# Rows of a pass sent as soon as a buffer is free, the temperature as a factor of q's way out of its bank, and four last pieces split

## The reference, cut to what matters

```
x = norm(x + attention0(x))    # 16 heads of 8 channels, over all 1024 keys
x = norm(x + quantised_matmul(x))
x = norm(x + attention1(x))    # 16 heads of 8, layernorm of q and k, rope, causal
x = norm(x + ffn(x))           # silu(x Wg) * (x Wu), then Wd, hidden 384
```

```
q = l2norm(q) * scale;  k = l2norm(k) * scale
attn = softmax((q @ k.T) / temperature)
```

## Time and profile before

| | |
|---|---|
| time, median of 3 runs | 862.54 us (862.5 to 862.57) |
| profiled execution: its own time | 866.08 us |
| profiled execution: span from first to last instruction | 864.4 us |
| TensorE matmuls busy | 831.2 us, 96% |
| ScalarE busy | 771.8 us, 89% |
| VectorE busy | 550.9 us, 64% |
| GpSimd busy | 150.1 us, 17% |
| mean granted TensorE clock | 0.989 of full |

### The profile page before, as it was taken

One profiled execution on the slowest core, in us unless ns is written; L12 is line 12 of the kernel. 1 busy time (PEld: TensorE's weight loads), 2 busy tenths in 40 slices (PEclk: granted clock), 3 DMA queues, 4 the chain that ended last, 5 costly groups with the idle time before them and its releaser, 6 DMA issues.

```text
span 864.4 us, 16509 instructions
## 1 busy us (share of the span) xinstructions
PE 831.2 (96%) x6266; PEld 307.4 (36%) x6268; DVE 550.9 (64%) x1459; ACT 771.8 (89%) x864; POOL 150.1 (17%) x352
## 2 busy tenths in 40 slices
PE   8899999999999899999999999999999999989995
PEld 4232333333333333333333433343333443434444
DVE  6264666668758567787672576765563476765656
ACT  4899999999999799899899999999999998979851
POOL 3000000000001400034100410023200442352210
PEclk9999999999999899999999999999999999989998
DMA  5755513314432611352340321142140330062000
GB/s 152 246 160 184 171 38 115 105 37 158 161 122 76 218 38 61 111 184 74 134 160 25 111 98 38 61 160 74 38 159 25 98 112 25 26 221 85 1 13 27
DMA packets 48565, 88.60 MB, mean 103 GB/s; under 512 B 5088, under 2 KB 14432, under 8 KB 48480
## 3 DMA queue, kind: packets, MB, share of 16 engines
q1 hardware_dynamic: 48000, 87.00, 29.9%
q10 hardware_dynamic: 480, 0.48, 0.2%
HBM read 51.03 MB, written 35.65 MB: 100 GB/s over the span
## 4 chain that ended last, share of the span: by engine, by line
PE 80%; DVE 11%; DMA 3%; issue 3%; SPq 2%; ACT 1%; POOL 1%; DVEq 0%; ACTq 0%; POOLq 0%
PE ps L907 39%; PE ps L885 24%; PE ps L853 5%; PE ps L864 3%; PE ps L860 3%; PE ps L779 3%; DMA q_st<-parts_scratch 2%; PE ps L838 2%; ACT probs L757 1%; DVE th L1310 1%; DVE hT L1311 1%; SPq L540 1%; DVE sums_t L1151 1%; DVE mid_part L1300 1%; DVE mid_part L1301 1%
## 5 line engine op out<-in xcount | busy, mean ns | idle before, releaser
L757 ACT ACTIVATE probs<-ps 128x1024 f32<-128x1024 f32 x800 | 751.7, 1073 | 58.3 <-PE ps L885 55.6
L907 PE MATMUL ps<-probs,v_st 128*32 128x512 f32 (+3 forms) x3584 | 430.4, 562 | 3.4 <-issue 1.2
L885 PE MATMUL ps<-q_st,k_st 32*128 32x512 f32 (+3 forms) x1792 | 269.7, 462 | 7.8 <-DMA q_st<-parts_scratch 5.2
L885 PEld LDWEIGHTS ps<-q_st,k_st 32*128 32x128 f32 x1792 | 123.7, 184 | 251.1 <-ACT probs L757 157.4
L673 POOL TENSOR_SCALAR_AFFINE_SELECT probs<-probs 128x256 f32<-128x256 f32 x256 | 108.6, 444 | 152.1 <-ACT probs L757 150.7
L907 PEld LDWEIGHTS ps<-probs,v_st 128*32 128x32 f32 x3584 | 76.4, 109 | 112.1 <-issue 79.3
L655 POOL COPY v_st<-v_all 128x256 f32<-128x256 f32 (+1 forms) x65 | 28.3, 437 | 404.4 <-PE ps L907 396.5
L1151 DVE STREAM_TRANSPOSE sums_t<-ps 128x512 f32<-128x512 f32 x32 | 22.9, 716 | 44.0 <-PE ps L907 43.5
L1285 DVE COPY mid_qkv<-ps 128x384 f32<-128x384 f32 x32 | 17.8, 558 | 38.4 <-PE ps L853 35.6
L860 PE MATMUL ps<-yTp,w_hid 128*128 128x512 f32 x84 | 30.8, 448 | 4.4 <-DVE hT L1311 1.5
L1285 DVE COPY prep_qkv<-ps 128x384 f32<-128x384 f32 x24 | 13.4, 558 | 30.9 <-PE ps L853 30.8
(11 more groups left out here) (188 smaller groups left out, 634.0 us busy)
## 6 DMA issues: line engine op xcount, KB each, us to landing
k_st<-parts_scratch SPq DMA_DIRECT2D x47, 512.0 KB, 3.5
parts_scratch<-mid_part SPq DMA_DIRECT2D x36, 512.0 KB, 3.9
q_st<-parts_scratch SPq DMA_DIRECT2D x63, 256.0 KB, 4.2
parts_scratch<-prep_part SPq DMA_DIRECT2D x28, 512.0 KB, 4.0
k_st<-parts_scratch SPq DMA_DIRECT2D x16, 256.0 KB, 2.8
xT<-in_xT SPq DMA_DIRECT2D x8, 256.0 KB, 5.0
x_all<-in_x SPq DMA_DIRECT2D x8, 256.0 KB, 5.6
out<-yo SPq DMA_DIRECT2D x7, 256.0 KB, 2.4
```

The source lines that it names most:

```text
L757: nc.scalar.activation(probs[:, k % PS, :, 0:w], slot(k)[:, :, 0:w], ACT.Exp).then_inc(probs_ready, 1)
L885: last_ = mm(slot(k)[:, e, at:at + n], k_st[row, p % KB, kt * P:(kt + 1) * P], q_st[row, p % KB, lo:HALF], start=True, stop=not shifted)
L907: last_ = mm(acc[HR * h:HR * (h + 1), lo:HALF], v_st[:, p % VB, kt, h, :], probs[:, (2 * s + h // 2) % PS, h % 2, at:at + n], start=FIRST[ ...
```

## The change

- **Rows.** There are four buffers of rows (KB = 4) in place of three. The entry of a pass in SyncE's list moves from slot "last step of p - 3, plus 1", priority 3, to slot "last step of p - 4, minus 1", priority 0; the parts of q and k that a pass needs still bound it by slot s + 1, priority 3. To make room, `w_hid_i` is laid over `hT` and `squares` over `attn`.
- **Temperature.** The piece `temp` and the table `tfac` are gone, and `temp` is gone from the planner's lists. A new input `tcol` holds each channel's temperature, one number for each of the 128 partitions; after q's transpose a channel is a partition. The two instructions that read q out of its bank multiply by `tcol`: the copy becomes a `tensor_scalar`, the subtraction a `scalar_tensor_tensor`. `mid` chunks are as before.
- **Head.** ScalarE issues `small` ahead of `w_qkv`, and `tcol` as a third load; VectorE waits for both small loads. ScalarE, not VectorE, writes the high part of q of chunk 0, and VectorE only the low part.
- **End.** Two of the four left pieces stay ahead of the loop over j, and two come after it.

```
-KB = 3
+KB = 4
...
-       [("dve", n, 0) for n in ("square", "norms", "rs1", "rs2", "scale", "temp")] + QKT
+       [("dve", n, 0) for n in ("square", "norms", "rs1", "rs2", "scale")] + QKT
...
-            todo.append((max([LAST_STEP[p - KB] + 1 if p >= KB else 1] + [s + 1 for s in parts]), 3, "rows", p, None))
+            todo.append((*max([(LAST_STEP[p - KB] - 1, 0) if p >= KB else (1, 3)] + [(s + 1, 3) for s in parts]), "rows", p, None))
...
+            act.dma_start(small[:], a["small"].partition_broadcast(P)).then_inc(small_in, 16)
             act.dma_start(w_qkv[:, 0, :], a["w0_qkv"]).then_inc(w_in, 16)
-            act.dma_start(small[:], a["small"].partition_broadcast(P)).then_inc(small_in, 16)
+            act.dma_start(tcol[:], a["tcol"]).then_inc(small_in, 16)
...
+            act.wait_ge(tcol_made, 1)
+            act.wait_ge(head_turned, 2)
+            nc.scalar.activation(job["prep"]["part"][:, 0, 0, :], head_bank[0], ACT.Copy, scale=tcol[:]).then_inc(head_high, 1)
...
-            dve.wait_ge(small_in, 16)
+            dve.wait_ge(small_in, 32)
...
-            ch.link(ts(tfac[:], bc(temp.unsqueeze(2), [P, H, D]), 1.0 / D, None, ALU.mult))
+            ch.link(v.reciprocal(tcol[:], tcol[:]))
+            ch.link(ts(tcol[:], tcol[:], 1.0 / D, None, ALU.mult))
+            dve.sem_inc(tcol_made, 1)
+            ch.link(ts(temp, temp, 1.0 / D, None, ALU.mult))
...
-            units(LEFT)
+            units(LEFT[:LEFT_FIRST])          # LEFT_FIRST = 2
             for j in range(NJ):
...
+            units(LEFT[LEFT_FIRST:])
...
+                if name == "prep" and k == 0:
+                    ch.link(ts(part[:, 0, 0, :], side, tcol[:], None, ALU.mult))
+                    stt(out=part[:, 0, 1, :], in0=side, scalar=tcol[:], in1=part[:, 0, 0, :].bitcast(F32), op0=ALU.mult,
+                        op1=ALU.subtract).then_inc(side_read, 1)
...
-                rows_norm("prep", c, "temp")
-                for u in (1, 0):
-                    dve.wait_ge(head_turned, 2 - u)
-                    part = job["prep"]["part"]
-                    chain["prep"].link(v.tensor_copy(part[:, u, 0, :], head_bank[u]))
-                    chain["prep"].link(tt(part[:, u, 1, :], head_bank[u], part[:, u, 0, :].bitcast(F32), ALU.subtract))
-                    dve.sem_inc(parts_ready["prep"], 1)
+                part, ch = job["prep"]["part"], chain["prep"]
+                dve.wait_ge(head_turned, 1)
+                ch.link(v.tensor_copy(part[:, 1, 0, :], head_bank[1]))
+                ch.link(tt(part[:, 1, 1, :], head_bank[1], part[:, 1, 0, :].bitcast(F32), ALU.subtract))
+                dve.sem_inc(parts_ready["prep"], 1)
+                dve.wait_ge(head_high, 1)
+                ch.link(stt(out=part[:, 0, 1, :], in0=head_bank[0], scalar=tcol[:], in1=part[:, 0, 0, :].bitcast(F32),
+                            op0=ALU.mult, op1=ALU.subtract))
+                dve.sem_inc(parts_ready["prep"], 1)
```

More of the change, by code:

```diff
@@ L146 @@
 DVE_US = {"ln_stats": 0.9, "ln_aggr": 0.8, "ln_out": 1.2, "ln_out_x": 1.2, "ln_out_y": 1.2, "amax": 1.2, "quant": 1.0,
-          "round": 1.0, "ffn_bias": 0.75, "add": 0.75, "square": 1.7, "norms": 1.3, "scale": 1.3, "temp": 0.75,
+          "round": 1.0, "ffn_bias": 0.75, "add": 0.75, "square": 1.7, "norms": 1.3, "scale": 1.3,
           "rope0": 1.3, "rope1": 1.5, "rope2": 1.3, "rope3": 1.3, "weights": 2.8, "centre": 1.5, "rot": 2.0,
@@ L165, in act_time @@
     return 2 * (0.12 + 2 * STEPS[s][2] * 0.00077)
-FIRST_KEYS = [("prep", 1, "pe", "qkT", 1), ("prep", 1, "dve", "scale_q", 0), ("prep", 1, "dve", "temp", 0),
-              ("prep", 1, "pe", "qkT", 0)]
+FIRST_KEYS = [("prep", 1, "pe", "qkT", 1), ("prep", 1, "dve", "scale_q", 0), ("prep", 1, "pe", "qkT", 0)]
 BRANCHED = 7
@@ L281 @@
 SIDE_ORDER, JOBS = side_order()
+LEFT_FIRST = 2
 LEFT = [(j["name"], j["c"], *u) for j in JOBS for u in j["left"]]
@@ L379, in program @@
     w_ffn = sb("w_ffn", [P, C], BF16)
-    w_hid_i = sb("w_hid_i", [P, 3, HID], I32)
     w_hid = sb("w_hid", [P, 2, HID], F32R)
@@ L388, in program @@
     rot = sb("rot", [P, 3, KT, 2, D], F32)
-    tfac = sb("tfac", [P, H, D], F32)
+    tcol = sb("tcol", [P, 1], F32)
     ident = sb("ident", [P, P], F32)
@@ L414, in program @@
     warm = sb("warm", [P, HALF], BF16)
-    squares = sb("squares", [P, C], F32)
     job = {}
@@ L433, in program @@
     yT = sb("yT", [P, HALF], F32)
+    squares = attn[:, 0:C]
     yTp = sb("yTp", [P, PARTS, HALF], F32R)
@@ L439, in program @@
     hT = sb("hT", [P, NJ, HALF], F32)
+    w_hid_i = hT[:].bitcast(I32).rearrange("p j s -> p (j s)")[:, 0:3 * HID].rearrange("p (n c) -> p n c", n=3)
     th = sb("th", [P, 2, HALF], F32)
@@ L469, in program @@
     warm_ready, head_qkv, norms_ready = sem("warm_ready"), sem("head_qkv"), sem("norms_ready")
+    tcol_made, head_high = sem("tcol_made"), sem("head_high")
     head_turned, end_filled, h_ready, end_down = sem("head_turned"), sem("end_filled"), sem("h_ready"), sem("end_down")
@@ L730, in square @@
                         act.wait_ge(norms_ready, done)
-                    nc.scalar.activation(squares[:], ps[:, c * TC + t, u * C:(u + 1) * C], ACT.Square,
+                    nc.scalar.activation(squares, ps[:, c * TC + t, u * C:(u + 1) * C], ACT.Square,
                                          accum_out=buffers("prep", c)["st"][:, 0, 2 * t + u:2 * t + u + 1]).then_inc(norms_ready, 1)
@@ L1015, in flags @@
             m, t = cst[:, 0, :], cst[:, 1, :]
-            ch.link(v.tensor_reduce(m[:, 0:1], tfac[:].rearrange("p h d -> p (h d)"), AX.X, ALU.max,
+            ch.link(v.tensor_reduce(m[:, 0:1], temp, AX.X, ALU.max,
                                     apply_absolute_value=True))
@@ L1120, in rows_norm @@
                 if name == "prep":
-                    dve.sem_inc(qk_ready[name], 1)
+                    dve.sem_inc(qk_ready[name], 2)
             elif what in ("scale_q", "scale_k"):
@@ L1125, in rows_norm @@
                            bc(per(1)[:, :, u].unsqueeze(2), [P, TC, C]), ALU.mult))
-                if u:
-                    dve.sem_inc(qk_ready[name], 1)
-            elif what == "temp":
-                ch.link(tt(out[:, :, 0:C], out[:, :, 0:C],
-                           bc(tfac[:].rearrange("p h d -> p (h d)").unsqueeze(1), [P, TC, C]), ALU.mult))
                 dve.sem_inc(qk_ready[name], 1)
@@ L1171, in piece @@
                 later_consts(what, k)
-            elif what in ("square", "norms", "rs1", "rs2", "scale", "scale_q", "scale_k", "temp", "rope0", "rope1", "rope2", "rope3"):
+            elif what in ("square", "norms", "rs1", "rs2", "scale", "scale_q", "scale_k", "rope0", "rope1", "rope2", "rope3"):
                 rows_norm(name, c, what)
@@ L1299, in read @@
                     dve.wait_ge(rows_in[0], 32 * PRODUCTS)
-                ch.link(v.tensor_copy(part[:, k, 0, :], side))
-                tt(part[:, k, 1, :], side, part[:, k, 0, :].bitcast(F32), ALU.subtract).then_inc(side_read, 1)
+                if name == "prep" and k == 0:
+                    ch.link(ts(part[:, 0, 0, :], side, tcol[:], None, ALU.mult))
+                    stt(out=part[:, 0, 1, :], in0=side, scalar=tcol[:], in1=part[:, 0, 0, :].bitcast(F32), op0=ALU.mult,
+                        op1=ALU.subtract).then_inc(side_read, 1)
+                else:
+                    ch.link(v.tensor_copy(part[:, k, 0, :], side))
+                    tt(part[:, k, 1, :], side, part[:, k, 0, :].bitcast(F32), ALU.subtract).then_inc(side_read, 1)
                 got()
@@ L1418 @@
                                  g["L1_attn_q_beta"], g["L1_attn_k_beta"]]),
-        "rope": rope_table(),
+        "tcol": np.repeat(g["L0_attn_temperature"].reshape(H), D)[:, None], "rope": rope_table(),
     }
```

## The result

The changed kernel takes 859.0 us (median of 18 runs, 857.76 to 862.32), the kernel before, in 18 runs of its own, 865.48 us (862.5 to 869.59). The ratio is 0.992 (95% interval 0.9905 to 0.9934): 0.8% faster, 6.5 us. I had forecast 9.5 us and 853.0 us, with a range of 850 to 858. The direction is right, the gain is 3 us short. Another 2.9 us of the miss in the absolute time come from the base: the three runs of before that were shown had 862.54, its median over all runs is 865.48. On the base of 862.54 the measured gain would have given 856.1, inside my range; on the measured base the time lies 1 us above it.

What follows compares the result with a forecast made beforehand. ScalarE's exps, or TensorE's work in slots with a side piece, bound the kernel, so only waits could yield gains: 0.4 + 3.7 + 3.2 + 2.2 + 0 = 9.5 us, 862.5 to 853.0 us, range 850.0 to 858.0.

Steps and rivals of the forecast that it cites:

- Late rows: Passes 19 and 58, near 290.77 and 763.45 us: both waits and their clock dips go, gaining 3.7 and 3.2 us.
- End: After the last exps: two pieces move behind the loop, TensorE's 2.21 us wait for hT goes, gaining 2.2 us.
- Temperature beside the exps: Side pieces on VectorE: removed instructions were hidden, replacements add nothing; taken as 0, plus or minus 2.6 us.
- The planner's new order: Side pieces after slot 18 possibly elsewhere, their number the same; taken as 0, plus or minus 2.6 us.
- Head: Start up to the first scores: 0.7 us gained less 0.3 gives 0.4 us, bounds -0.1 and 0.9.
- 0, the middle: Start of VectorE's constants in the head: between 0.45 us late and 0.45 early, taken as 0.
- The other terms: In the head: 0.7 us gained without `temp`, 0.3 us lost to a longer chain of constants.
- without a pause until pass 1's rows: SyncE's issues in the head: no pause, so the 0.7 us from removing `temp` carries through.
- The sum: Whole kernel: 0.4 + 3.7 + 3.2 + 2.2 + 0 = 9.5 us gained.
- The base: Whole kernel: median of runs 862.5 us, 3.5 us below the profiled time, a difference kept for the forecast.
- Rival 1: One stall stays or a new late operand appears with a clock dip, costing some 3.7 us: 856.7 us; chance 0.14.
- Rivals 2, 3 and 4: Row edit does nothing, 859.9 us, 0.07; slower, 864 or more, 0.05; new order wins waits, below 850.5, 0.08.

Runs made afterwards that it cites:

- small_first: The kernel before with ScalarE's first two loads exchanged (`small`, then `w_qkv`), no `tcol`: 868.05 us, ratio 1.0016.
- end_only: The kernel before with only the split of the four left pieces at the end: 863.54 us, ratio 0.9979.
- temp_head_only: The kernel before with the temperature's edit and the new head, overlaid tiles as in the changed kernel: 867.58 us, ratio 1.0025.
- changed_third: The changed kernel itself, run a third time: 858.91 us, ratio 0.993; its profiled execution takes 856.4 us.
- rows_end: The kernel before with the row edit and the split of the last pieces, old head and temperature: 857.1 us, ratio 0.9896; repeat 856.54 us, 0.9896.
- w_first: The changed kernel with `w_qkv` issued ahead of `small` again, `tcol` third: 858.64 us, ratio 0.9922; repeat 858.77 us, 0.9919.
- rows_only: The kernel before with the row edit alone (four buffers, new place in SyncE's list, two overlaid tiles): 856.06 us, ratio 0.9901.
- kb4_old_slots: The changed kernel with four buffers but the rows at their old kind of place in SyncE's list: 859.64 us, ratio 0.9915.

## Why the prediction was right and wrong

- **Late rows: right, somewhat too small.** 4.4 and 3.8 us in place of 3.7 and 3.2. Both lie above my upper bounds (3.89 and 3.36). These were ScalarE's idle time alone, in the windows. Without a wait its exps start 0.92 us apart though each takes 1.02, and every idle piece costs this overlap too. With four such pieces in the first stretch and three in the second I estimate 0.4 and 0.3 of the missing 0.5 and 0.45 us from it. How much a late row costs also varies: by the same ruler the second cost 1.9 to 2.9 us in the three other profiles that still have it (`small_first`, `end_only`, `temp_head_only`), the first 3.8 to 4.4, so the profile of before that both forecast and comparison rest on is the dearest of four. The rows go at 277.3 us, 274.2 on the clock of before (the steps there start 3.1 us later), where I had 274. What I named as the mechanism isn't its only form: the buffer or the place alone does it.
- **End: right against this profile.** 2.4 for 2.2. hT's first block, the wait that goes and VectorE as what comes last are as worked out. But 1.5 of the 2.4 are the down matmuls at the low clock, and two of the four profiles with the old end don't have that; there the new end is worth 0.9. Alone it measures 1.8 us with an interval that includes none, and on top of the rows nothing that can be told.
- **Temperature beside the exps: nearly.** I had taken the replacement for nothing from rows of 0.688 and 0.691 us without a per-partition factor. They take 0.75, and cost 0.6 us, since not VectorE's busy time counted but how long it holds the bank for TensorE's next piece. The planner's new order costs little, as I took: outside the late rows the exps of `changed_third` lose 0.15 us against before from step 12 to 352, those of `rows_end`, which keeps the old order, gain 0.64; of the 0.79 between them the reads are 0.60, which leaves 0.2.
- **Head: wrong, and the step that failed.** I took "0, the middle" of ±0.45 us for the start of the constants. They start 1.78 us late, at 7.98, since `tcol` lands at 7.96 only. As the third load behind `small` and `w_qkv` its 0.5 KB took 6.2 us; my bounds, from loads of 16 and 24 KB, were 3.8 and 4.9. The Trainium skill (DMA: Bandwidth & Descriptors, "Anatomy of one DMA") has about 2.0 us fixed plus the bytes, as a fit for DMAs that GpSimd issues. ScalarE issued this one, and here the measured 6.2 us decides. The other terms came out: 0.7 for `temp`, 0.3 for the longer chain. What I had left out altogether is that the change moves `w_qkv` one place later too, and TensorE waits for it. In the changed kernel's own profile that wait is covered by `tcol`'s; in `small_first` it costs 1.2 us by itself, and where the clock falls behind it more. Instead of a gain of 0.4 the head costs 1.1 us, 1.6 in the mean of the profiles. With `w_qkv` first again it is 0.1 (`w_first`), since `tcol` lands at 6.97 and takes back what `temp` gave. That SyncE issues "without a pause until pass 1's rows" was a misreading: in before it stands still from 29.04 to 32.37 us, until the two stores have landed. The copy with a pointer operand on ScalarE takes 0.69 us for 0.59, which agrees with what the prediction quoted for it.
- **The sum.** Rows and end alone: forecast 9.1, measured 9.4 and 9.2 us in two sets of runs. Temperature and head: forecast a gain of 0.4, measured a loss of 2.2 alone and 2.3 in the whole. That is 2.7 of the 3.0 us that are missing. The traces show the late first exp (1.6 us in the mean of the profiles) and the reads (0.6) in it. As times of whole kernels these two are not shown: the exchange of loads measures 1.3 us alone, with an interval that just includes none. That `w_first` and `w_first_again`, without the exchange, are not below the changed kernel stays unexplained; their medians scatter with pass 1's two forms, and both profiles fell on the worse one.
- **The base.** "The median lies 3.5 us below the profiled one's time; I keep that difference": with more runs it fell to 0.6 (865.48 and 866.08), and stood at 1.2 after the change. The three runs that were shown lie below all of the other fifteen (862.96 to 869.59). This step moved the absolute time by 2.9 us, more than temperature and head together did (2.7 us); with the base as shown the time would lie in the range.
- **Rival 1** (a new late operand with a clock dip) is near to what the profile after shows at pass 1, though I had it from rows or the new order of pieces. But this stretch comes and goes in one kernel, with or without the change. What stays open is why SyncE's issue of the two stores takes 1.25 to 1.4 us in most profiles and 1.9 to 2.5 in the others. Rivals 2, 3 and 4 are excluded: no wait for late rows, no waits in SyncE's order, no gain beyond.

## What to carry to other kernels

When a change reorders the first loads, price each load that changes place, and each new one behind it, by who waits for it, and take a landing time from a load in the same place, not from one of the same size. An instruction that reads a bank costs what it holds the bank for the writer behind it, even where its engine has 36% idle. And before explaining a difference of one or two profiles, look for stretches at half clock behind the same wait: here they come and go between executions of one kernel and are worth 1.5 to 3 us each, which is more than some parts of a change; in one kernel (`rows_end`) a few matmuls on zeros in such a wait took 1.2 us off the time and most of its scatter, though they held the scores up for 2.2 us after the data was there. A part whose worth was read behind such a stretch, like the new end, may bring nothing once another part is in.

## What the runs showed of the hardware that was not expected

- A load of 24 KB to 128 partitions from one row, issued 0.45 us ahead of one of 192 KB, makes this land 2.4 us later and another queue's load of x 1.3 us later (`small_first`), and lands 0.16 us earlier itself. One of 0.5 KB, issued third by ScalarE at 1.74 us, takes 6.2 us to land behind these two and 5.2 with the larger one first (`w_first`).
- VectorE with a per-partition factor: 751 ns for 128x512 out of a bank, against 691 without. ScalarE: 0.69 us against 0.59 (two different copies of this size).
- The granted clock fell behind pass 1's wait in all nine profiles where it was 2.6 to 3.2 us long, behind one of 1.42 us (`rows_end`), and behind 0.77 and 1.29 us apart (`kb4_old_slots`); it stayed up behind 0.75 and 1.28 (`changed_third`) and 1.04 and 1.14 (before). Behind the wait of 1.25 us near 729 us it fell in some profiles of a kernel and not in others. Behind the same wait of 2.2 us in the old end, the first eight down matmuls take 2.08 us (before) or 1.16 (`rows_only`). Short waits thus have no fixed price.
- SyncE's issue of the same two stores takes 1.25 to 1.4 us or 1.9 to 2.5 us, and with the longer one the following rows are issued 5.2 to 5.8 us after its start instead of 6.3 to 6.7.
